# Two heads at a time in the last attention of a four-stage decoder kernel

## What is computed

```python
# cross attention: q = x, k = v = ctx; 16 heads, 8 channels each
qh = (q @ Wq + bq).reshape(B, 256, 16, 8).transpose(0, 2, 1, 3)
kh = (k @ Wk + bk).reshape(B, 256, 16, 8).transpose(0, 2, 1, 3)
vh = (v @ Wv + bv).reshape(B, 256, 16, 8).transpose(0, 2, 1, 3)
attn = softmax(einsum('bhqd,bhkd->bhqk', qh, kh) * 8 ** -0.5)
x = layernorm(x + einsum('bhqk,bhkd->bhqd', attn, vh).concat() @ Wo + bo)
# experts: 2 of 8 for each token, at most 40 places in each expert and batch
probs = softmax(x @ Wr); topk_probs, topk_experts = top_k(probs, 2)
pos = running count of the tokens of each expert
buf[expert, batch, pos] = x, where pos < 40
y = relu(buf @ W1 + b1) @ W2 + b2
x = layernorm(x + sum over the two experts of prob * y[expert, batch, pos])
```

## Time and profile before

| what | value |
|---|---|
| three runs | 787.52, 790.64, 794.8 us, median 790.64 us |
| profiled execution | 796.1 us, of which the span of instructions is 794.3 us |
| instructions | 16402 |
| PE, DVE, ACT, POOL busy | 91%, 62%, 52%, 37% of the span |
| granted TensorE clock, mean | 0.937 of full speed |

### The profile page before, as it was taken

The page is one execution under the profiler, slowest core; times in us unless marked ns, Lnnn a source line. Parts: engine busy times, 40 slices in busy tenths (PEclk is TensorE's granted clock), DMA queues, the critical chain, the costliest instruction groups (busy, mean ns, idle before and its releaser), DMA issues.

```text
span 794.3 us, 16402 instructions
## 1 busy us (share of the span) xinstructions
PE 719.1 (91%) x5852; PEld 542.2 (68%) x5852; DVE 489.1 (62%) x1297; ACT 412.9 (52%) x1047; POOL 290.0 (37%) x395
## 2 busy tenths in 40 slices
PE   8788889898897998999999989989888899999886
PEld 6565567575665765899898967758566455767665
DVE  4669777887977885444543455545455658583643
ACT  2234556657566677554544467555562545454311
POOL 0015355565555666110000036423350646363300
PEclk8869989999999999999999999999998756999999
DMA  8537451533727471000000000001011501000000
GB/s 235 126 69 179 123 128 43 122 83 88 161 46 205 112 214 57 2 1 1 1 1 1 1 1 4 1 2 41 4 38 54 185 26 31 2 2 9 8 7 7
DMA packets 25175, 48.11 MB, mean 61 GB/s; under 512 B 7264, under 2 KB 14192, under 8 KB 25096
## 3 DMA queue, kind: packets, MB, share of 16 engines
q1 hardware_dynamic: 24376, 45.66, 22.7%
q10 hardware_dynamic: 720, 1.41, 0.5%
HBM read 17.49 MB, written 0.52 MB: 23 GB/s over the span
## 4 chain that ended last, share of the span: by engine, by line
PE 60%; DVE 14%; issue 10%; ACT 8%; SPq 3%; POOL 2%; DMA 2%; POOLq 0%; ACTq 0%; DVEq 0%
PE SC L839 7%; PE G L550 7%; PE SC L826 7%; PE SC L769 5%; PE G L625 4%; PE SC L861 3%; PE G L938 3%; DVE shift_cols L1542 3%; PE SO L812 3%; ACT causal_probs L1154 2%; PE SO L893 2%; PE SC L743 2%; PE G L647 2%; SPq L1769 1%; PE G L577 1%
## 5 line engine op out<-in xcount | busy, mean ns | idle before, releaser
L1169 ACT ACTIVATE exps<-SC 128x512 f32<-128x512 f32 x192 | 114.4, 597 | 106.8 <-PE SC L769 106.1
L1542 DVE TENSOR_REDUCE shift_cols<-SC 128x2 f32<-128x512 f32 x192 | 129.5, 684 | 32.0 <-PE SC L743 31.5
L1621 POOL TENSOR_TENSOR rstd<-variance,consts 128x2 f32<-128x2 f32 (+1 forms) x48 | 36.8, 766 | 266.0 <-DVE variance L1234 263.0
L1689 POOL TENSOR_TENSOR VB<-exps 128x256 f32<-128x256 f32 x128 | 95.7, 756 | 59.4 <-ACT exps L1169 58.6
L1143 ACT ACTIVATE hidden<-SC,cols 128x256 f32<-128x256 f32 x128 | 53.6, 471 | 65.4 <-PE SC L826 65.3
L1711 POOL TENSOR_TENSOR causal_probs<-causal_probs,inverse 128x256 f32<-128x256 f32 x64 | 51.6, 828 | 68.9 <-DVE inverse L1555 68.9
L1576 DVE SCALAR_TENSOR_TENSOR R<-SC,small,R 128x128 f32<-128x128 f32 x128 | 39.0, 346 | 54.0 <-PE SC L839 53.3
L1154 ACT ACTIVATE causal_probs<-SC,negmax 128x128 f32<-128x128 f32 (+1 forms) x128 | 52.3, 424 | 37.1 <-DVE negmax L1550 37.0
L769 PE MATMUL SC<-stacked_q,stacked_k 100*128 100x256 f32 x256 | 66.9, 344 | 3.5 <-DMA stacked_q<-shift_rows 1.9
L839 PEld LDWEIGHTS SC<-ffn_w,hidden 128*128 128x128 f32 x512 | 66.0, 192 | 5.3 <-issue 1.8
L839 PE MATMUL SC<-ffn_w,hidden 128*128 128x128 f32 x512 | 67.6, 276 | 0.0
(11 more groups left out here) (257 smaller groups left out, 1504.5 us busy)
## 6 DMA issues: line engine op xcount, KB each, us to landing
stacked_k<-k_hi SPq DMA_DIRECT2D x64, 128.0 KB, 2.4
stacked_q<-q_hi SPq DMA_DIRECT2D x64, 128.0 KB, 2.4
ffn_w<-in_ffn_w SPq DMA_DIRECT2D x16, 512.0 KB, 4.8
stacked_k<-k_lo SPq DMA_DIRECT2D x32, 128.0 KB, 2.4
stacked_q<-q_lo SPq DMA_DIRECT2D x32, 128.0 KB, 2.5
packed_k<-U SPq DMA_DIRECT2D x48, 32.0 KB, 1.9
packed_q<-YN SPq DMA_DIRECT2D x48, 32.0 KB, 1.9
a_weights<-in_a_li SPq DMA_DIRECT2D x3, 256.0 KB, 7.4
```

Of the source, the lines that this page charges most:

```text
L1169: fn(exps[:, n % EXPS, :, :].rearrange("p t q -> p (t q)"), SC[1][:, n % 2, :, :].rearrange("p t q -> p (t q)"), ACT.Exp, scale=ATTENTIONS ...
L1542: v.tensor_reduce(shift_cols[:, n // UNIT % 4, :, n % UNIT], SC[0][:, n % 2, :, :], axis=AX.X, op=ALU.max, negate=True).then_inc(head_max, 1)
L1689: v.tensor_tensor(kept[n % EXPS].rearrange("p t q -> p (t q)"), exps[:, n % EXPS, 0, :], exps[:, n % EXPS, 1, :], ALU.add).then_inc(kept_r ...
```

## The change

In the cross attention (heads 128 to 191), and nowhere else, each even slot takes two heads. `cross_products` issues for each tile of 128 rows four matmuls in a row: score products of heads n and n+1, transposed products of heads n-10 and n-9. These four heads lie in four different groups of rows. It waits for the maximum of all heads before n and for the exponential of all heads before n-10, since a pair now fills both banks of SC[0], or of SC[1]. DVE reduces two heads in one instruction (128x1024 in), ACT takes one exponential of 128x1024, POOL adds 128x512.

The shift is turned in the unit's slot +4 instead of +6 and used at +10 instead of +9. The values are laid out with the 8 channels of each of a batch's 16 heads in their own partitions, with zeros around them (`cross_values` writes into tiles that POOL clears once, `clear_values`), and a batch's 16 heads are accumulated in one tile of SO. Its other half takes the sums, through a matrix of ones for each unit (`cross_sum`). So the logarithm, the guess, the check, the refinement and the division run once per batch instead of once per unit, and `project_out` has one matmul for each token tile instead of four. There is one such tile of SO, so the first sum and values of a batch wait for the division of the batch before. The division is at slot +19 of the batch's last unit, `mix` starts at 32 instead of 31, and its steps behind the norm stand two slots later.

```diff
-LAST = LX_AT + HEADS * (NB - 1) + OUT_AFTER + 31
+LAST = LX_AT + HEADS * (NB - 1) + CROSS_OUT_AFTER + 33
+SHIFT_LAG, CROSS_LAG = 9, 10
+CROSS_TURN_AT = 4
+CROSS_INVERT, CROSS_REFINE, CROSS_DIVIDE = 18, 19, 19
...
+                def cross_products(n, m):
+                    if n is not None:
+                        if n == STACK_HEADS:
+                            pe.wait_ge(exp_ready, NB * PAIRS)
+                            pe.wait_ge(key_ones_in, 16 * 2)
+                        pe.wait_ge(head_max, n)
+                        if n % UNIT == 0:
+                            pe.wait_ge(packed_in[n // UNIT % 4], 16 * 6 * (stream_of(n) % NB + 1))
+                    if m is not None:
+                        pe.wait_ge(head_exp, m)
+                        if m % UNIT == 0:
+                            pe.wait_ge(shifts_in[m // UNIT % 4], 16 * (m // UNIT // 4 + 1))
+                    for t in range(TT):
+                        of = slice(t * P, (t + 1) * P)
+                        if n is not None:
+                            for h in (n, n + 1):
+                                q, kk = packed(h, HD - 1)
+                                last = mm(SC[0][:, h % 2, t, :], q[:, of], kk, start=True, stop=True)
...
+                        if m is not None:
+                            for h in (m, m + 1):
+                                q, kk = packed(h, HD)
+                                last = mm(SC[1][:, h % 2, t, :], kk[:, of], q, start=True, stop=True)
...
+                def cross_place(b):
+                    if b == 0:
+                        wait_emptied(pe, ("OC", 4 * NB - 1))
+                    else:
+                        pe.wait_ge(cross_divided, CROSS_UNIT + b)
...
-                    if at["d"] == HD:
+                    if s // NB == LX:
+                        c0, chunks = 4 * (s % 2), 1
+                        pe.wait_ge(cross_divided, CROSS_UNIT + s % NB + 1)
...
-                    yield 5
+                    yield 7
                     normal_transposed(b, 8, X[b])
-                    yield 6
+                    yield 8
...
-                    yield 12
+                    yield 14
                     pe.wait_ge(chosen_ready[b], 2)
...
-                    yield 15
+                    yield 17
                     pe.wait_ge(dispatch_ready[b], 1)
...
+                def cross_refine(b):
+                    dve.wait_ge(inverse_checked, CROSS_UNIT + b + 1)
...
+                def cross_divide(b):
+                    dve.wait_ge(cross_outputs, CROSS_UNIT + 4 * (b + 1))
+                    dve.wait_ge(sums_inverse, CROSS_UNIT + b + 1)
...
+                    if slot in (LX_AT - 2, LX_AT + 6):
+                        clear_values(0 if slot < LX_AT else 1)
```

299 lines of the change are left out of this document (206 added, 93 removed).

## The result

| | median, us | runs | lowest to highest |
|---|---|---|---|
| before | 795.39 | 20 | 787.52 to 800.31 |
| changed | 803.51 | 20 | 792.20 to 813.19 |

The ratio is 1.0065 with a 95% interval of 1.0036 to 1.0095; the two medians alone stand at 1.010. A difference of two ratios is therefore the safer size where the two disagree. The change made the kernel slower. The prediction, 773.0 us and 758 to 789, was wrong, in its sign too.

A forecast was written before the change was run, and what follows sets the result against it. PE was taken as the bound in both middle stretches, cross attention alone and with experts. Terms summed to -17.6, say -18 us: 796.1 to 778.1 us for the profiled execution, scaled to 773; range 758 to 789.

The forecast's parts named there:

- Products four at a time: PE's cross attention products: four heads' run in the time of two, halving 42.15 us; -19.6 us.
- Output projection: PE's projection pieces after the cross attention: two records instead of eight per token tile; -7 us.
- Shifts turned earlier: Shift DMAs get six slots instead of three before use, so PE's wait for them goes; -1.5 us.
- One pair in both banks: PE must wait for DVE to read the last pair; gaps open where no experts run; +5 us, bounds 0 and 12.
- POOL's add: POOL's 128x512 addition per pair, 1.04 to 1.54 us, ends inside the same gap as DVE's reduction; no added cost.
- Sums, guesses, divisions: Done once per batch, 13 us of refinements and divisions leave DVE, which isn't the bound; counted 0.
- SP: SP's queue of packing DMAs: faster slots lengthen ACT's wait before the next batch's queries; +2 us, bounds 0 and 5.
- Steps behind the norm later: Dispatch, refinement and division in one piece on DVE delay what follows, 1.2 us for each of three batches; +3.5 us.
- The clock at its present share: PE's granted clock left unchanged; in the stretch of cross attention alone, bounds of 11 us saved to 10 us lost.
- rival C: The clock falls beside the experts, each us at half clock costing one more; 802 us scaled, chance 0.07.
- rival B: Reading out becomes the bound: every pair, also beside the experts, pays a gap; +8 us, 781 scaled, chance 0.18.
- marks named for being wrong: Expert stretch not shrinking about 10 us, PE's DVE or ACT waits over 12 us, or clock beside experts leaving 1.00.

The follow-up runs named there:

- e19: The changed kernel with POOL's addition of a pair's key tiles split into two instructions of 128x256, nothing else; 793.3 us, ratio 0.9970.
- e3: The changed kernel with a second set of the unpacked tensors for batches 1 and 3; 807.0 us, ratio 1.0141.
- e6: The changed kernel with the edits of both e1 and e3; 797.9 us, ratio 1.0021.
- e4: The kernel before with only the steps behind the norm moved two slots later; 800.0 us, ratio 1.0079.
- e1: The changed kernel with the steps behind the norm back at their old slots, two earlier; 798.4 us, ratio 1.0030.
- e15: The changed kernel, later steps kept, with the second set of unpacked tensors and 107 fillers (matmuls on zeros) in PE's idle time; 794.3 us, ratio 0.9985.
- e2: The changed kernel with six matmuls on zeros before PE's wait for each dispatch; 807.1 us, ratio 1.0156.
- e11: The kernel before with 24 matmuls on zeros where its profile shows PE idle; 796.7 us, ratio 1.0027.
- e8: The kernel before with the pairs alone (products, maxima, exponentials, key tile sums of two heads at once, lag 10); 798.7 us, ratio 1.0030.

## Why the prediction was wrong

By its own steps:

- *Products four at a time*, -19.6: right, -20.1 in the profile, 0.44 us for a block.
- *Output projection*, -7: from 10.4 us (64 records) to 5.0 (16), -5.4. The records that are left take 410 ns instead of 312, some of them at half clock.
- *Shifts turned earlier*, -1.5: the wait is gone.
- *One pair in both banks*, +5: this step failed. It counted the reduction (1.2, measured 1.222) and the hand-over between pairs (0.3 to 0.8 us each, as worked out), and nothing else that stands in DVE's queue. Before the change PE ran a head ahead of DVE, so a normalisation, a dispatch or queries and keys in DVE's order hid behind one bank. With pairs PE stops at each of them: 14.7 us of waits for maxima against the 5, half of them at two places, 4.6 and 2.8 us.
- *POOL's add*, priced at nothing as its end lies in the gap: this failed too. Its length also sets how long some of DVE's instructions stand still. No other single edit to the changed kernel gave as much as its split: 10.2 us in the medians, 7.6 by the ratios (e19), though only 1.7 once idle time was filled.
- *Sums, guesses, divisions*, 0, "this free time pays for what follows": the free time was there (DVE is busy 114 of 215 us), but not where the chain was. DVE had also a little less of it before than the prediction read, 32% of the first stretch and not a third.
- *SP*, +2 with a bound of 5: 7.9 with the clock held, nothing measurable without (e3, e6). The step looked at how long ACT waits, not at who stands behind DVE.
- *Steps behind the norm later*, +3.5: 4.3 alone on the kernel before (e4), 5.1 in the changed kernel or 2.8 by the ratios (e1), 8.4 with the clock held (e15). Somewhat too small.
- *The clock at its present share*: failed. It fell beside the experts, which the prediction had as rival C at 0.07 with the price "each us at half costs one more". Rival C is what happened in this profile, 34 us at half clock in two falls. In the medians the half-clock time rose by 14 us, some 5 us of time, and at equal half-clock time the kernel is still some 4 us slower, so C is about half of the loss and not the whole. Its reason was mis-sized as well: I had the clock hang on the kind of matmul, and idle time at the dispatches counted as a wait of 1.2 us each and not as something that can take the clock with it.

Added up in medians, from part to part: before 795.4, with the output tile alone 792.6 (-2.8, predicted -8.5), with pairs and lag 10 798.4 (+5.8, predicted -12.6), with the later steps 803.5 (+5.1, predicted +3.5). By the ratios the three steps are -2.8, +5.2 and +2.8. Either way the mistake is in the pairs. With the clock held, the steps back and the second set they are worth 5.3 us, a quarter of the products' 20. That DVE's loop is then the bound, as in rival B, fits its length (1.22 us for the reduction and 0.64 from the first product to its start, 632.39 to 633.03), but is argued and not shown: the fillers stand in the gaps that would show it.

Of the marks named for being wrong all three came: the stretch with the experts grew by 9.4 us, PE's waits for DVE and ACT passed 12 us (14.7 for the maxima alone), and the clock beside the experts fell to 0.87.

## What to carry to other kernels

Work taken from the engine that bounds is worth only what the next engine's in-order queue lets through: before two steps are joined so that they share all buffers, list everything that stands in that queue between them, at its longest duration. Joining instructions on an engine nobody waits for is not free either, if another engine stands still for as long as one of them lasts; keep them short. And after a change that makes the busiest engine lighter, look at its idle stretches and the clock behind them before the busy sums.

## What was not expected of the hardware

- *DVE beside POOL.* A normalisation of 128x128 took 0.34 us alone, up to 0.87 beside POOL's additions of 128x256, and up to 1.46 beside those of 128x512; the reductions from PSUM stayed at 1.22 us beside either. The Trainium skill (SBUF — State Buffer, SBUF: two separate sides) says that GpSimd's instructions and those of DVE in a two-port mode or with two SBUF inputs take a shared port pair as an exclusive lock for a whole instruction, and that the other engine blocks. The traces agree: 2.57 us became 1.44 by shorter instructions of POOL alone. Whether the normalisation, which has one such input, ran in a two-port mode, no run here shows.
- *The clock.* It fell to 1.2 GHz behind two gaps of PE, 1.44 and 2.27 us with 1.98 us of work between, and behind a single one of 2.04 us, and stayed there for 17 us in which PE was busy 16.74 of 17.1. A gap alone doesn't say how long a fall lasts, or that one comes. The same wait of 2.04 us for a dispatch stands in the kernel before, and there the fall was over in 3.4 us:

```profile
768.42 1.86 PE L923 MATMUL G<-slot_of,X 128*128 128x512 f32 x2 [2.04 <-DVE slot_of L1510]
768.70:772.10 3.40, 3.29 (x4) 0.69 (x3) 1.51 (x4) 0.07 (x1) 0.00 (x0) 0.50 0.13 39
```

In e2, with the first of the two gaps filled, the second was still 2.26 us, and no fall came:

```profile
719.71 1.64 PE L1016 MATMUL G<-no_context 128*128 128x144 f32 x12
721.29 1.98 PE L1019 MATMUL G<-slot_of,X 128*128 128x512 f32 x4
725.53 0.46 PE L672 MATMUL G<-w_lx_wo,OB 128*128 128x128 f32 x2 [2.26 <-issue]
```

The Trainium skill (TensorE: Matmul & The Clock Gate, HAM oscillation) warns of longer idle gaps than these. Where idle time was filled with matmuls on zeros, half-clock time in the median went from 107 to 66 and 53 us. The kernel before also has falls with PE busy nearly all the time, where single heads' products prevail (3.40 of 3.4 us ahead of the fall at 669.7), and fillers took only some 11 us off its half-clock time (e11).
- What stands ahead of the first pair is nearly the same in all kernels, and took between 589.9 us (e8, clock 0.97) and 600.2 us (e2, 0.96) in their profiled executions. So one profiled execution doesn't tell a per cent.
